# Sending sorted edges from one core: a written-out GpSimd program, dealt over nine stages instead of five

## What is computed

```python
edge_index = jnp.stack([src, dst])            # edges come sorted by dst
xn = _layernorm(x)
x = x + gnn0(xn, edge_index) + mix0(xn)       # two rounds of: sum relu(x[src]) over dst, then an MLP; linear attention
x = x + ffn0(_layernorm(x))                   # one 256 x 256 product and a bias
xn = _layernorm(x)
x = x + gat1(xn, edge_index) + mix1(xn)       # graph attention summed over src; elu attention with rmsnorms
x = x + moe1(_layernorm(x))                   # 8 experts, the best 2 for each node
```

## Time and profile before

| | |
|---|---|
| median of 3 runs | 6463.12 us (6459.19 to 6470.74) |
| the profiled execution, its own time | 6463.77 us |
| its span, from the first to the last instruction | 6461.3 us |
| POOL busy | 3605.4 us, 56%, 3729 instructions |
| PE busy | 3358.7 us, 52% |
| DVE busy | 2820.4 us, 44% |
| ACT busy | 1933.3 us, 30% |
| DMA packets of GpSimd's queue | 142720 |

### The profile page before, as it was taken

One profiled execution on the slowest core, in us unless ns is written; L12 is line 12 of the kernel. 1 busy time (PEld: TensorE's weight loads), 2 busy tenths in 40 slices (PEclk: granted clock), 3 DMA queues, 4 the chain that ended last, 5 costly groups with the idle time before them and its releaser, 6 DMA issues. The chain is left out here.

```text
span 6461.3 us, 79625 instructions
## 1 busy us (share of the span) xinstructions
PE 3358.7 (52%) x13479; PEld 2417.8 (37%) x13480; DVE 2820.4 (44%) x7047; ACT 1933.3 (30%) x4744; POOL 3605.4 (56%) x3729
## 2 busy tenths in 40 slices
PE   3455555555365666667440825056666650409991
PEld 0134444444344444445320725034444440306660
DVE  4645555432144444444331325555555557502223
ACT  0133333333233333332110301055555541103331
POOL 0056666666766666665676777277777750050005
PEclk9567777778777777778775968578888875559995
DMA  2133333333133333333100211011111130351114
GB/s 71 39 115 93 93 93 94 93 95 57 25 100 101 99 100 100 100 97 42 26 1 4 49 15 27 3 26 27 27 27 27 27 21 0 129 190 52 55 55 126
DMA packets 280598, 407.39 MB, mean 63 GB/s; under 512 B 93991, under 2 KB 197765, under 8 KB 280262
## 3 DMA queue, kind: packets, MB, share of 16 engines
q0 software_dynamic: 142720, 275.10, 18.4%
q1 hardware_dynamic: 137798, 131.50, 6.6%
HBM read 323.82 MB, written 81.61 MB: 63 GB/s over the span
## 5 line engine op out<-in xcount | busy, mean ns | idle before, releaser
L1075 PE MATMUL conv_ps<-conv_msg,conv_S 128*128 128x256 f32 x3328 | 1200.9, 535 | 996.7 <-DMA conv_msg<-relu_xn_table,GI 534.4
L1075 PEld LDWEIGHTS conv_ps<-conv_msg,conv_S 128*128 128x128 f32 x3328 | 905.0, 281 | 1319.9 <-issue 1128.8
L1047 DVE TENSOR_TENSOR ACC<-ACC,conv_ps 128x256 f32 x1664 | 700.2, 421 | 1195.3 <-PE conv_ps L1075 1092.5
L998 POOL DMA_INDIRECT conv_msg<-relu_xn_table,GI x832 | 800.0, 962 | 570.1 <-issue 235.2
L998 POOL DMA_INDIRECT conv_msg<-conv_table,GI x832 | 788.8, 948 | 379.8 <-issue 235.8
L1766 POOL DMA_INDIRECT gat_msg<-attn_table,GI x832 | 825.5, 992 | 266.9 <-issue 253.2
L1819 PE MATMUL gat_ps<-gat_M,gat_S 128*128 128x260 f32 x1664 | 597.1, 509 | 377.7 <-DVE ACC L1873 229.0
L1018 ACT ACTIVATE conv_S<-iota_row,LOC 128x128 f32<-128x128 f32 x1664 | 507.9, 388 | 894.8 <-PE conv_ps L1075 806.5
L1819 PEld LDWEIGHTS gat_ps<-gat_M,gat_S 128*128 128x128 f32 x1664 | 379.9, 247 | 518.8 <-issue 462.4
L2411 POOL DMA_INDIRECT combine_y<-expert_out,combine_at x98 | 94.1, 960 | 578.4 <-ACTq L2399 559.9
L818 POOL DMA_INDIRECT edges_by_src<-mlp_lanes_pay,mlp_lanes_idx x288 | 341.6, 1186 | 109.7 <-issue 76.8
(11 more groups left out here) (388 smaller groups left out, 5330.3 us busy)
## 6 DMA issues: line engine op xcount, KB each, us to landing
expert_in<-router_zrow SPq DMA_DIRECT2D x53, 256.0 KB
experts_xe<-expert_in SPq DMA_DIRECT2D x106, 128.0 KB
expert_out<-experts_y SPq DMA_DIRECT2D x106, 128.0 KB, 1.7
conv_msg<-relu_xn_table,GI POOLq DMA_INDIRECT x832, 2.7
conv_msg<-conv_table,GI POOLq DMA_INDIRECT x832, 2.7
gat_msg<-attn_table,GI POOLq DMA_INDIRECT x832
relu_xn_table<-norm_rx SPq DMA_DIRECT2D x49, 128.0 KB, 1.7
xnT<-norm_xt SPq DMA_DIRECT2D x49, 128.0 KB
```

The lines of the kernel that those rows point to most:

```text
L998: pool.indirect_dma_start(msg[:, h * RING + k, :], None, table, bass.IndirectOffsetOnAxis(ap=m.GI[:, t:t + 1], axis=0)).then_inc(got[h] if ...
L1047: nc.vector.tensor_tensor(acc, acc, ps[k % NB][:, 0:D], ALU.add).then_inc(added, 1)
L1075: nc.tensor.matmul(ps[k % NB][:, 0:D], S[:, h % 2, k, :], msg[:, h * RING + k, :], start=True, stop=True).then_inc(summed, 1)
```

## The change

A new function `send_columns` takes the place of `Scatter.columns` for the order by source. It writes out one indirect DMA for each column in Python, with no loop on the engine, takes the index straight from `m.rank_i[:, j:j + 1]` and the values straight from `m.packed[:, j:j + 1]`, and has no copies. Two semaphores alternate between groups of eight. Ahead of the third and each later group GpSimd waits until the group two back has landed, and at the end for the last two.

The 800 columns are dealt anew: `mlp1` 136, `mix` 8, `mlp2` 144, `stats1` 16, `ffn` 80, `stats2` 16, `akv` 152, `aq` 160, `aadd` 88. (`Scatter` stays for the sort by target, which runs only where the edges don't come sorted.)

```diff
+def send_columns(nc, m, pool, sent, first, count):
+
+    edges = m.edges[1].rearrange("(e a) -> e a", a=1)
+    for g in range(count // 8):
+        if g >= 2:
+            pool.wait_ge(sent[g % 2], g // 2 * 128)
+        for j in range(first + g * 8, first + g * 8 + 8):
+            pool.indirect_dma_start(edges, bass.IndirectOffsetOnAxis(ap=m.rank_i[:, j:j + 1], axis=0),
+                                    m.packed[:, j:j + 1], None).then_inc(sent[g % 2], 16)
+    for g in range(max(count // 8 - 2, 0), count // 8):
+        pool.wait_ge(sent[g % 2], (g // 2 + 1) * 128)
...
-def stage_stats(nc, m, name, eps, with_rms=False):
+def stage_stats(nc, m, name, eps, with_rms=False, columns=None):
...
+        sent = st.sems("sent")
         block = st.block()
+
+        if columns:
+            @block.gpsimd
+            def _(pool):
+                send_columns(nc, m, pool, sent, *columns)
...
-def stage_mix(nc, m):
+def stage_mix(nc, m, columns):
...
+        @block.gpsimd
+        def _(pool):
+            send_columns(nc, m, pool, sent, *columns)
...
-        scatter = Scatter(nc, m, st, 1)
+        sent = st.sems("sent")
...
-            scatter.columns(pool, *columns)
+            send_columns(nc, m, pool, sent, *columns)
...
-    stage_mlp(nc, m, "mlp1", m.w11s, m.b11s, m.w12s, m.b12r, False, (0, 144))
+    stage_mlp(nc, m, "mlp1", m.w11s, m.b11s, m.w12s, m.b12r, False, (0, 136))
...
-    stage_mix(nc, m)
+    stage_mix(nc, m, (136, 8))
     stage_mlp(nc, m, "mlp2", m.w21s, m.b21s, m.w22s, m.b22r, True, (144, 144))
-    stage_stats(nc, m, "stats1", 1e-5)
-    stage_ffn(nc, m, (288, 176))
-    stage_stats(nc, m, "stats2", 1e-5, with_rms=True)
-    stage_attn_kv(nc, m, (464, 176))
-    stage_attn_q(nc, m, (640, 160))
-    stage_attn_add(nc, m)
+    stage_stats(nc, m, "stats1", 1e-5, columns=(288, 16))
+    stage_ffn(nc, m, (304, 80))
+    stage_stats(nc, m, "stats2", 1e-5, with_rms=True, columns=(384, 16))
+    stage_attn_kv(nc, m, (400, 152))
+    stage_attn_q(nc, m, (552, 160))
+    stage_attn_add(nc, m, (712, 88))
```

More of the change, by code:

```diff
@@ L1657, in _, with stage_attn_add @@
             skewed(v, 2, step)
-def stage_attn_add(nc, m):
+def stage_attn_add(nc, m, columns):
     with Stage(nc, "aadd") as st:
```

## The result

The changed kernel takes 6238.72 us (median of 3 runs, 6235.86 to 6238.92) against 6463.12 before: ratio 0.9653, 95% interval 0.964 to 0.9666. The forecast was 6242.

A forecast was written before the change was run, and what follows sets the result against it. POOL was taken to bound the five sending stages and, after the change, all nine: 1460.5 - 1235.3 = 225.2 us, less 4 for DVE contention, gives 221 off 6463.12, so 6242 us (-3.4%), range 6222 to 6290.

The forecast's parts named there:

- What bounds the kernel: POOL ends the five stages that send columns, computing the other four; the nine stages take 1460.5 us before the change.
- Copies go: In the five sending stages, 95 group boundaries cost 0.305 instead of 1.24 us: 89 us, plus 3 at the openings.
- Columns move: 128 of 800 columns go to four stages where POOL idled: 191 us off five stages, 58 given back.
- DVE beside POOL: The 120 columns in stats1, stats2 and aadd may pay 29 to 60 ns, 3 to 7 us; 4 added.
- A: In the nine stages a column costs what a gather costs, 1.25 us: 6045 us; chance 5%.
- B: In stats1, stats2 and aadd POOL gets through only when DVE is done: up to 6360 us; chance 6%.
- B's milder case: In stats1, stats2 and aadd each of 120 columns waits one DVE instruction, 0.42 us: 50 us; most of B's 6%.
- C: In stats1, stats2 and aadd each DVE instruction waits for POOL's DMA: 288 us more, 6530 us; chance 2%.
- D: In the nine stages POOL's order holds but tails and new program cost more: 6250 to 6290, inside the forecast's 86%.

The follow-up runs named there:

- experiment 7: Changed kernel with aadd's tile work replaced by rows of three DVE forms, and 104 columns in conv2; scatters 188 ns longer beside scalar_tensor_tensor, 13 beside products.
- experiment 1: Kernel before with the written-out program without copies, columns dealt as before: 6365.57 us beside 6463.49 (0.985), ratio 0.9865 beside 7029, 1.0001 beside 7160.
- the probe: Changed kernel with one more stage at its end, sending eight scatters each of several shapes into scratch arrays; adds some 117 us, only its rows count.
- deal alone: Changed kernel with the two copies and their wait put back ahead of each group of eight: 6969.74 us beside 7160, 6836.3 beside 7029.
- columns in conv2: Changed kernel with 104 columns sent in conv2, taken from mlp1, mlp2, ffn and aadd: 7158.31 us beside 7160, 6944.06 beside 7029.
- short stages empty: Changed kernel with the 40 columns of mix, stats1 and stats2 sent in akv instead: 7075.46 us, ratio 0.9884, beside 7160.
- experiment 6: Changed kernel with each scatter sending 128 partitions instead of 125: 7377.66 us beside 7029, 6093.44 us beside 6461.73.

## Why the prediction was right

**What bounds the kernel.** Right: all nine stages end with POOL, and the sum of the nine was forecast at 1235.3 + 4 and measured at 1238.5.

| stage | mlp1 | mix | mlp2 | stats1 | ffn | stats2 | akv | aq | aadd |
|---|---|---|---|---|---|---|---|---|---|
| forecast | 207.1 | 16.5 | 219.3 | 28.5 | 123.9 | 28.5 | 231.2 | 244.5 | 135.8 |
| measured | 205.5 | 15.4 | 219.3 | 27.7 | 125.6 | 28.2 | 230.8 | 243.9 | 142.1 |

**Copies go.** Right, and shown alone: 97.9 us against 92. Between the DMAs of the five stages it is 91.2, where the sum had 89; most of the rest, 4.6 us, lies behind `aadd`, in stages that the sum left out.

**Columns move.** Right: 126.9 us, the difference of two runs, against 129. No stage fell back on its computing, and no gap stood at each eighth DMA. The tails were 3.1 us behind `mlp1` (3.9 forecast), 4.15 behind `mlp2` (4.2), 5.2 behind `aq` (5.5) and 4.8 behind `aadd` (4.2).

**DVE beside POOL.** The size was about right as a whole, by luck, and wrong in place. I spread 4 us over `stats1`, `stats2` and `aadd` at 29 to 60 ns a column; in the two `stats` stages a column took 1178 and 1179 ns, no more than alone, and of these three stages only the tile loop of `aadd` stretched them. Groups of POOL there, beside the statistics (3824 to 3841) and beside the tiles (3842 to 3920):

```profile
L845 POOL DMA_INDIRECT edges_by_src<-packed,rank_i x12 | 14.1, 1179 | 9.3 <-PEq L46 5.9 <-issue 3.4
...
L845 POOL DMA_INDIRECT edges_by_src<-packed,rank_i x49 | 64.2, 1310 | 14.9 <-issue 14.9
```

49 x 131 ns = 6.4 us, the whole of what `aadd` took over its forecast of 135.8. The prediction sized it by how densely DVE works; what the instructions are and where their operands lie sets it. `aadd` has one scalar_tensor_tensor with all operands in SBUF for each tile:

```profile
L1723 DVE SCALAR_TENSOR_TENSOR aadd_t<-aadd_t,aadd_r,ACC 128x256 f32<-128x256 f32 x49 | 23.8, 485 | 7.8 <-issue 7.6
L1721 DVE TENSOR_TENSOR aadd_t<-ACC,mw2r 128x256 f32<-128x256 f32 x49 | 20.7, 422 | 0.1
L1725 DVE TENSOR_TENSOR X<-X,aadd_t 128x256 f32 (+1 forms) x48 | 20.4, 426 | 7.8 <-issue 7.7
```

It is 37% of DVE's busy time in these rows, so experiment 7 gives an estimate of 0.37 x 188 + 0.63 x 13 = 78 ns, not 131. A scatter of 1.2 us always meets at least one of them, which may be why; that isn't shown. The figure of the Trainium skill ("SBUF — State Buffer", section on the two separate sides) that the prediction weighed, some 620 ns stretched to 3100, is for a DMA beside a VectorE `tensor_copy`. None of the DVE instructions timed here is one, so these runs neither show nor refute it; the longest mean beside any of them is 1368 ns against 1180, beside scalar_tensor_tensor.

**The rivals.** A, that a column costs what a gather costs, failed for the reason given: 125 partitions; of the two differences named there, the 4 bytes turned out to be none. With 128 partitions rival A's figure of 6045 was nearly reached (6093). B's sign was a mean of over 1.3 us in `aadd`: over the stage it was 1251 ns (110.13 us for 88), though 1310 beside the tiles; one DVE instruction waited for at each column, B's milder case, would have given 1.6 us. C would have stretched DVE: its 203 instructions in `aadd` took 80.67 us, where they took 80.62. D gave less than 2 us a stage.

**What was not foreseen.** The stages outside were to keep their lengths to 1 us; they gave 2.1 lost ahead of `mlp1`, and 2.5 won in `conv2` and 5.1 behind `aadd`. The program alone (experiment 1) gained 4.6 behind `aadd` too, so that comes with the new program and not with the deal; why stays open. That the total came within 3 us is in part luck: the nine stages were 3.2 us over the list of the forecast, `aadd` 6.3 and `ffn` 1.7 over and the others 4.8 under, and 4 us had been added for something else. And the forecast is for the condition of its own runs: beside 7029 and 7160 us the changed kernel itself was not run, and there its two parts gave 96 and 0 us for the program, 193 and 191 for the deal.

## What to carry to other kernels

If an engine sends transfers in the cover of computing, deal them by how long each stage computes, stages without any included, and take the price of one and the tail of a stage from the trace: nine stages came out within 2 us each but `aadd`, which was 6 over. Before counting how many transfers there are, try their shape: three partitions that carry nothing took 18% off each scatter. And run a kernel whose stages are balanced this finely more than once, beside the old one: 128 partitions gave -5.7% in one series and +5% in another.

## What the runs showed of the hardware

**A price by the number of partitions.** 0.94 us on 112, 0.96 on 128, 1.18 on 125, whatever the bytes.

**Landing of small scatters to adjacent places.** In the probe the engine waited 6.94, 6.43 and 6.12 us for eight scatters of 4 bytes to land (128, 125 and 112 partitions), 1.44 and 1.59 for 16 bytes, and 1.73 for 1024.

**Beside a denser stream of scatters the loops of other engines are longer, in some series.** The time from the first to the last matmul into `mlp_po` in `mlp1`, 49 tiles of the same work:

| kernel before takes | 6462 to 6463 | 7029 | 7160 |
|---|---|---|---|
| with copies between groups | 150.4 (kernel before) | 153.7 (deal alone) | 169.3 (deal alone) |
| 125 partitions, no copies | 150.9 (changed kernel), 150.5 (program alone) | 174.0 (program alone), 171.4 (columns in conv2) | 225.3 (program alone), 219.5 (short stages empty), 203.6 (columns in conv2) |
| 128 partitions, no copies | 150.6 | 315.9 | not run |

In the first column the stream doesn't matter; in the other two the computing gets slower as less time lies between the scatters and as each gets shorter. With that the copies' removal could be worth nothing beside 7160 us: beside the same 136 columns the loop took 169.3 us with copies (deal alone) and 219.5 without (short stages empty). That their pauses let the others through is the likely reading and isn't shown. The chip isn't what tells the columns apart: the third run of experiment 1 and the run of experiment 7 were on the same one, with the kernel before at 6463 us beside the one and at 7046 beside the other, so the word "chip" in my expectations was wrong. What does, and what the engines wait for in the 30 us of experiment 6, stays open.
